# The bias of a recurrence: from the tanh's operand to a one-row fp32 matmul per chunk

## What is computed

```
xw = jnp.einsum('ntd,dh->nth', x, Wx) + b
def step(prev_h, xw_t):
    next_h = jnp.tanh(xw_t + prev_h @ Wh)
...
h1 = jnp.einsum('bth,efh->btef', x, w1) + b1
h1 = jax.nn.gelu(h1, approximate=False)
expert_outputs = jnp.einsum('btef,ehf->bteh', h1, w2) + b2
```

## Time and profile before

| what | value |
|---|---|
| median of 3 runs | 351.78 us (351.67 to 352.82) |
| the profiled execution's own time | 354.47 us |
| its span, first to last instruction | 352.7 us |
| mean granted TensorE clock | 0.917 |
| busy: PE, DVE, ACT, POOL | 263.1, 313.4, 215.3, 156.4 us |

### The profile page before, as it was taken

One profiled execution on the slowest core, in us unless ns is written; L12 is line 12 of the kernel. 1 busy time (PEld: TensorE's weight loads), 2 busy tenths in 40 slices (PEclk: granted clock), 3 DMA queues, 4 the chain that ended last, 5 costly groups with the idle time before them and its releaser, 6 DMA issues.

```text
span 352.7 us, 8394 instructions
## 1 busy us (share of the span) xinstructions
PE 263.1 (75%) x2587; PEld 191.2 (54%) x2587; DVE 313.4 (89%) x648; ACT 215.3 (61%) x429; POOL 156.4 (44%) x186
## 2 busy tenths in 40 slices
PE   3778440002994996998779999788999989786894
PEld 3633140001454874787457777565777666563683
DVE  4798999897993889789999899999889999999985
ACT  5378898381523775576446676565667655584592
POOL 1459953494020147104771116786110766629500
PEclk9999865555797899899999999999999999999999
DMA  7963430000048000000000000000001000001000
GB/s 209 320 218 62 90 89 0 0 0 0 0 51 189 3 0 0 0 3 18 0 0 0 2 2 25 1 0 0 0 2 32 0 0 0 3 1 33 0 2 22
DMA packets 28074, 12.13 MB, mean 34 GB/s; under 512 B 17369, under 2 KB 26898, under 8 KB 28050
## 3 DMA queue, kind: packets, MB, share of 16 engines
q1 hardware_dynamic: 27106, 11.24, 12.9%
q10 hardware_dynamic: 944, 0.59, 0.7%
HBM read 6.58 MB, written 1.05 MB: 22 GB/s over the span
## 4 chain that ended last, share of the span: by engine, by line
PE 37%; DVE 37%; issue 13%; POOL 5%; DMA 2%; ACT 2%; DVEq 2%; SPq 0%; ACTq 0%; POOLq 0%
PE bank L829 36%; DVE big L804 8%; DVE big L808 5%; DVE wyT L764 5%; DVE peak L632 3%; DVE peak L564 3%; DVE big L657 2%; POOL big L349 2%; POOL big L348 2%; DMA x_sb<-in_x 2%; DVE big L637 1%; DVE big L680 1%; DMA wt<-wyT 1%; DVE big L682 1%; DVE c L688 1%
## 5 line engine op out<-in xcount | busy, mean ns | idle before, releaser
L829 PE MATMUL bank<-wt,big 128*128 (+1 forms) x1536 | 115.8, 220 | 25.1 <-DVE big L808 15.7
L808 DVE TENSOR_TENSOR big<-big 128x384 f16<-128x384 f32 (+2 forms) x160 | 123.2, 777 | 9.9 <-ACT big L527 5.8
L829 PEld LDWEIGHTS bank<-wt,big 128*128 128x128 f16 x1536 | 97.1, 98 | 60.6 <-issue 37.4
L525 ACT ACTIVATE big<-bank,miscT 128x384 f32<-128x384 f32 (+2 forms) x160 | 96.4, 603 | 43.5 <-PE bank L829 39.3
L829 PE MATMUL bank<-big,wt 128*128 128x384 f16 (+2 forms) x480 | 110.4, 339 | 0.0
L360 POOL CAST big<-q 128x64 f16<-128x64 f32 x32 | 10.8, 339 | 128.6 <-ACT q L519 101.6
L804 DVE CAST big<-big 128x512 f16<-128x512 f32 (+2 forms) x112 | 57.3, 512 | 11.2 <-ACT big L525 10.0
L519 ACT ACTIVATE q<-bank,miscT (+1 forms) x112 | 30.7, 274 | 41.8 <-PE bank L829 40.4
L829 PEld LDWEIGHTS bank<-big,wt 128*128 (+1 forms) x480 | 46.6, 117 | 12.4
L829 PE MATMUL bank<-q,wxh 128*128 (+1 forms) x254 | 45.3, 254 | 5.4 <-ACT q L496 5.1
L829 PEld LDWEIGHTS bank<-q,wxh 128*128 128x128 f32 x254 | 39.5, 196 | 10.6 <-ACT q L496 7.0
(11 more groups left out here) (139 smaller groups left out, 294.0 us busy)
## 6 DMA issues: line engine op xcount, KB each, us to landing
wnat<-in_w SPq DMA_DIRECT2D x8, 512.0 KB, 7.4
x_sb<-in_x SPq DMA_DIRECT2D x4, 256.0 KB, 5.9
out_block<-wyT SPq DMA_DIRECT2D x16, 64.0 KB
b_all<-in_b SPq DMA_DIRECT2D x1, 512.0 KB, 4.8
wn<-in_w_gate ACTq DMA_DIRECT2D x1, 192.0 KB, 2.8
wn<-in_w_up ACTq DMA_DIRECT2D x1, 192.0 KB, 4.5
wn<-in_w_down ACTq DMA_DIRECT2D x1, 192.0 KB, 5.1
wt<-wyT SPq DMA_TRANSPOSE x8, 3.4
```

Of the source, the lines that this page charges most:

```text
L525: A(g32[:, f, 0:w], ps_h[f][:, 0:w], ACT.Gelu, bias=bias, scale=1 / WS).then_inc(g32_done, 1)
L808: V.tensor_tensor(g_lo[:, par, f, 0:w], g32[:, f, 0:w], g_hi[:, par, f, 0:w], ALU.subtract).then_inc(g_lo_done, 1)
L829: return nc.tensor.matmul(o, l, r, start=start, stop=stop, skip_group_check=True)
```

## The change

The bias leaves the tanh. Its scale stays a constant and its bias is now the constant 0. Instead, `input_part` ends with a fourth matmul into the same columns: the left side is the row of `misc` that holds `b` (partition 32), the right side a row of the new tile `ws_row`, filled with 256, so that 256 times `b` is added to each column. Both are fp32. POOL fills `ws_row` with a memset between two constants that PE waits for before its first instruction; the count that PE and POOL wait for goes up by one.

```diff
+        ws_row = sb("ws_row", [E * NF + 1, BANK])
...
+            G.memset(ws_row[:, :], WS).then_inc(consts, 1)
             G.iota(experts[:, :], [[1, E]], base=0, channel_multiplier=0,
                    allow_small_or_imprecise_dtypes=True).then_inc(consts, 1)
-            pool.wait_ge(consts, 2)
+            pool.wait_ge(consts, 3)
...
-            bias_h = miscT[:, SLOTS:SLOTS + 1]
...
-                A(h32[:, at], ps_rnn[:, at], ACT.Tanh, bias=bias_h, scale=1 / WS).then_inc(h32_done, 1)
+                A(h32[:, at], ps_rnn[:, at], ACT.Tanh, scale=1 / WS).then_inc(h32_done, 1)
...
                         A(h32[:, bass.ds(step * B, B)], ps_rnn[:, bass.ds(rnn_column(c, step), B)], ACT.Tanh,
-                          bias=bias_h, scale=1 / WS).then_inc(h32_done, 1)
+                          scale=1 / WS).then_inc(h32_done, 1)
...
-            pe.wait_ge(consts, 3)
+            pe.wait_ge(consts, 4)
...
             def input_part(first, to):
 
                 at = slice(B * first, B * to)
+                bias_at = E * NF
                 mm3(ps_rnn[:, 0:B * (to - first)], wx_hi[:, :], wx_lo[:, :], x1_hi[:, at], x1_lo[:, at])
+                mm(ps_rnn[:, 0:B * (to - first)], misc[bias_at:bias_at + 1, :], ws_row[bias_at:bias_at + 1, 0:B * (to - first)],
+                   False)
```

## The result

The changed kernel takes 359.38 us (median of 4 runs, 357.05 to 361.75), the kernel before 352.3 beside it: a ratio of 1.0199, 95% interval 1.0127 to 1.0272. That is 7.1 us slower where 2.6 were forecast, and the time is 3.3 over the range's upper end. A later set of 6 runs of the same kernel (changed_4) gave a ratio of 1.0166 (1.0134 to 1.0198), 5.9 us.

A forecast was written before the change was run, and what follows sets the result against it. The prediction saw no single bound, but PE on the chain at all five edited places. 3.41 us for the matmul less 0.34 and 0.43 for the tanh gave +2.64, from 351.78 to 354.4 us, range 352.6 to 356.1.

The forecast's parts named there:

- Where the work lies: All five places of the new matmul lie on PE, and PE is on the chain there.
- E (swallowed): The three chunk-start insertions fall into DVE's slack; only the first two stay: +0.6 us, 352.4, chance 0.06.
- D (faster): In the recurrence's ring 53 shorter tanhs count, 4.5 us against 3.41: -1.1 us, 350.7, chance 0.05.
- The price of a column: New fp32 matmul: two passes, 1.67 ns a column, 3.41 us over the five places.
- The memset: At the start on POOL: hidden under the transfer PE's first instruction waits for; cost nothing, without that cover under 1 us.
- The step that failed: At each of the five places the new matmul's two weight loads are covered: 0 taken, at most 0.2 us a place.
- The second step that failed: At the second place the clock rises at the same moment: net 0.64 us; 0.64 more if pushed back.
- The third, a term mis-sized: the tanh: Each tanh 0.085 us shorter, counting at four PE waits (0.34 us) and five tanhs in chunk 0 (0.43 us).
- Rival C: Clock rise pushed back, loads uncovered at five places, no ACT gain in chunk 0: +4.7 us, 356.5, chance 0.13.

The follow-up runs named there:

- late_only: The changed kernel with the one-row matmul only at the starts of chunks 1, 2 and 3; the first 40 steps keep the tanh's bias operand: 356.37 us, ratio 1.0107.
- rows128: The changed kernel with the fp32 bias matmul's weight tile of 128 rows, 127 of them zero, instead of one row: 355.4 us, ratio 1.0078 to the kernel before.
- first_only: The changed kernel with the one-row matmul only at the first place; tanhs after the first 16 keep the bias operand: 353.54 us, ratio 1.0032.
- second_only: The changed kernel with the one-row matmul only at the second place, before chunk 0; all other steps keep the operand: 353.67 us, ratio 1.0037; second trace's run 355.36.
- second_full: The changed kernel with 128 weight rows at the second place only, one row at the other four: 357.6 us, ratio 1.0127 to the kernel before.
- mm_only: The changed kernel with the bias operand back in the tanh, so the bias counts twice: 360.47 us, ratio 1.0229 to the kernel before.
- tanh_only: The kernel before with the tanh on constants and no bias at all: 352.38 us against 352.76, ratio 0.9990.
- rows128_2: The kernel rows128 once more, timed side by side with the changed kernel: 355.65 us, ratio 1.0071 to the kernel before.
- f16_rows: The changed kernel with the bias split into two fp16 rows, high and low part, added in one pass: 355.72 us, ratio 1.0061 to the kernel before.
- f16_rows128: The kernel f16_rows with its weight tile at 128 rows, 126 of them zero: 352.63 us, ratio 0.9999 to the kernel before.

## Why the prediction was wrong

**Where the work lies: right.** All five insertions are on the path; late_only pays 3.8 us (2.6 to 4.9) for three insertions of 3.2, and rivals E (swallowed) and D (faster) fell with it.

**The price of a column: right.** 1.67 ns, two passes: rows128 has 0.86 us between starts for 512 columns (forecast 0.85) and at the first place 0.43 (0.43). The memset took 0.52 us and PE's first instruction was still released by the transfer, at 3.86.

**The step that failed: "I take none, since the first can run under the fp16 matmul ahead and the second under the first pass".** I had kept up to 0.2 us a place for uncovered loads as a bound and took 0. The bound was too low as well, since it counted the new matmul's own two loads and not the one behind it. With 1 or 64 rows all three loads beside the matmul (one for each pass, one for the work behind it) stay uncovered, 0.1 us each at the high clock: 0.28 to 0.30 us a place, 0.4 at the place with the low clock, 1.6 in all. My own reasoning would have held for 128 rows, as rows128 shows; I had read no row of before with a load of few rows for it, and set the likeliest value at the end of the bound instead of between the two.

**The second step that failed: "if it rises at the same moment, what is pushed behind it runs at the full clock and the net is 0.64".** I let the rise be pushed back by the matmul's own length at most, 0.64 us. In three of the four traces of the changed kernel it comes 5 to 6 us later than in the fourth, which costs 1.6 to 1.8 us more in B, the 0.6 us for the bias columns at the low clock among them. The reading under it was wrong too: I took the clock to be up from 114.8, by the 0.17 us of matmuls of 8 columns, but in that trace it stood at 0.50 up to 116 and rose at about 116.7.

**The third, a term mis-sized: the tanh.** 0.77 us was forecast and 0.4 measured, with an interval that reaches from -0.3 to 1.0; the segments show none of it after chunk 0. Its length was read rightly (0.085 against 0.091). What isn't borne out is that it would count at the chunk starts and in five slots of chunk 0. Where a stretch has PE and ACT both without a gap, as the earlier trace rows has, a busy ACT doesn't say that ACT sets the pace.

**Rival C had the parts.** It named both the uncovered loads and the pushed-back rise, at 356.5 us and with a chance of 0.13. Its sizes were too small: 1.0 for loads that cost 1.6, 0.64 for the clock where the late course costs about 1.7, and it still took off 0.34 for the tanh.

**The sum anew, made after the fact:** 3.4 for the columns, 1.6 for the loads, 1.7 for the clock where it comes late, less 0 to 0.4 for the tanh: 6.3 to 6.7 in a late execution, 4.6 to 5.0 in an early one. Measured were 7.1 (4.5 to 9.6) and 5.9 (4.7 to 7.0), medians over executions of both kinds. Part by part, first_only, second_only and late_only add up to 1.1 + 1.3 + 3.8 = 6.2.

**What stays open.** That few rows at the second place put off the clock's rise rests on a count, 6 in 10 against 0 in 10, with the reservations above; it is likely and not shown. Why they would, and what decides between the two courses of one program, no run here shows. In second_full against the changed kernel the gain is 1.2 to 1.8 us with overlapping intervals. And mm_only is 1 to 2 us slower than the changed kernel, while its tanhs are off the path by tanh_only's measure; its B is 37.88 with the clock up latest of all. Its interval (1.0206 to 1.0252) overlaps the changed kernel's first one and lies above the second (1.0134 to 1.0198), so this excess may be real, and nothing here explains it. How the loads behave between 64 and 128 rows was not run, nor was one of the two sides alone cut down: weights and right side had the same number of rows in each kernel.

## What to carry to other kernels

A matmul that adds a row (a bias, a rank-one term) isn't priced by its columns alone: in a dense stretch a weight tile of few rows cost about 0.1 us here for each load beside it, and the same tile padded with zeros to 128 rows cost its columns alone (1.14 against 0.86 us at 512 columns). Over this kernel the padding was worth 3.15 us, of which the loads are 1.6 and the rest is in part the clock. Shortening an operation is worth only what another engine was waiting for: 128 tanhs shorter by 0.09 us gave nothing that could be told from zero, and ACT stood waiting for PE before most of its work both before and after. And before a sum is made on one profiled execution, see how it stands to the median, and in which segment: here 1.9 us of a long B were in it.

## What the runs showed of the hardware that was not expected

Weight loads of few rows weren't hidden behind the matmul ahead, for 1 and 64 rows in fp32 and for 2 rows in fp16, and neither was the load that follows such a matmul (1.14 and 1.15 against 0.86 us; 0.41 against 0.21). The Trainium skill, in TensorE: Matmul & The Clock Gate, section "LDWEIGHTS (loading the stationary operand)", says that a load of 32 rows takes the same time as one of 128, since only the columns count. The trace of the changed kernel agrees with that for the load's own length: 184 ns is the median of the ten one-row loads, 198 the mean of the 254 loads of the recurrence's fp32 weights of 128 rows. The section speaks of 32 rows, which no run here has. What differs by the rows here is whether the load is covered.

After PE's pause ahead of the second place, which ends at 109.1 to 111.8 us, the clock stands at 0.50. It rises at 112.5 to 117.9 us in all ten traces with 128 rows at the second place or no bias matmul there, and at 119.9 to 122.7 in 6 of 10 traces with a few-row matmul there.

Two programs that are equal over a stretch sometimes differ there by 1.1 us: C of rows128_2 is 48.72 against 47.58 in rows128, E of changed_4 is 103.66 against 102.45. In both the trace shows a granted clock of 0.50 where the other one has 1.00: in rows128_2 from about 169.1 to 172.5 and from 182.7 to 186.1 us, in changed_4 from about 310.2 to 313.6.

```profile
168.00:170.00 2.00, 1.08 (x10) 0.77 0.00 0
170.00:172.00 2.00, 2.00 (x15) 0.50 0.00 0
172.00:174.00 2.00, 2.00 (x23) 0.88 0.00 0
```

The first of these rows, of rows128_2, has PE busy for 1.08 of 2 us. f16_rows has two such stretches in C as well (from 169.1 and 182.8 us), and a C of 48.36 against 46.98 in f16_rows128. But late_only has one at about 176 us and a C of 47.81, no longer than others, so that the clock is the whole cause isn't shown.
